# Edge attention on Trainium2: dividing the softmax on the edges and building the attention table with the edge pairs stationary

## What is computed

```python
Xq = (H @ W_lin.T).reshape(bt, n, h, dh)      # 4 heads of 64
Xv = (H @ W_val.T).reshape(bt, n, h, dh)
e = einsum('behd,hd->beh', leaky_relu(Xq[:, src] + Xq[:, dst], 0.2), a)
e = e + log(A0[src, dst] + 1e-8)[None, :, None]
e_t = e.transpose(1, 0, 2)
m = segment_max(e_t, src)
ex = exp(e_t - m[src])
attn = ex / segment_sum(ex, src)[src]
Y = segment_sum(attn[..., None] * Xv[:, dst], src)
return Y.reshape(bt, n, d) @ W_out.T
```

## Time and profile before

| | us |
|---|---|
| median of 3 runs | 2039.13 (2038.29 to 2039.25) |
| the profiled execution | 2038.4 |
| its span on the core | 2036.5 |
| edge attention, within it | about 1130 to 1637 |
| mean granted clock of TensorE | 0.984 |

### The profile page before, as it was taken

The page is one execution under the profiler, slowest core; times in us unless marked ns, Lnnn a source line. Parts: engine busy times, 40 slices in busy tenths (PEclk is TensorE's granted clock), DMA queues, the critical chain, the costliest instruction groups (busy, mean ns, idle before and its releaser), DMA issues. The chain is left out here.

```text
span 2036.5 us, 32320 instructions
## 1 busy us (share of the span) xinstructions
PE 1954.2 (96%) x11918; PEld 1586.9 (78%) x11918; DVE 1239.6 (61%) x2612; ACT 990.0 (49%) x1619; POOL 191.4 (9%) x162
## 2 busy tenths in 40 slices
PE   7999999999999999999999799999999889897998
PEld 6998888888888889888888556757565678686998
DVE  7454665544454535545554577575664588897786
ACT  3554564333332324322323365472736255675996
POOL 1000000001101010011011060000000011100000
PEclk8999999999999999999999899999999999997999
DMA  3111001000100000100102321422314131001232
GB/s 120 51 33 42 0 0 42 0 0 0 41 1 1 0 0 1 32 1 4 79 0 80 117 84 63 137 94 80 119 45 144 32 104 62 23 0 52 84 103 94
DMA packets 81490, 99.97 MB, mean 49 GB/s; under 512 B 7408, under 2 KB 73584, under 8 KB 79088
## 3 DMA queue, kind: packets, MB, share of 16 engines
q1 hardware_dynamic: 81392, 98.65, 14.7%
HBM read 61.78 MB, written 33.55 MB: 47 GB/s over the span
## 5 line engine op out<-in xcount | busy, mean ns | idle before, releaser
L706 ACT ACTIVATE b_gate<-b_pG,b_bias 128x512 f32<-128x512 f32 (+2 forms) x460 | 294.9, 669 | 368.5 <-PE b_pG L55 367.6
L53 PE MATMUL b_pG<-b_xshi,b_whi 128*128 128x512 f32 (+2 forms) x920 | 351.6, 382 | 2.3 <-PEq L299 1.4
L54 PE MATMUL b_pG<-b_xslo,b_whi 128*128 128x512 f32 (+2 forms) x920 | 351.3, 382 | 0.0
L55 PE MATMUL b_pG<-b_xshi,b_wlo 128*128 128x512 f32 (+2 forms) x920 | 351.3, 382 | 0.0
L756 DVE CAST b_xshi<-HT 128x512 fp32r<-128x512 f32 (+3 forms) x130 | 57.4, 484 | 285.2 <-PE b_pG L55 268.5
L53 PEld LDWEIGHTS b_pG<-b_xshi,b_whi 128*128 128x128 f32 x920 | 172.7, 188 | 35.7 <-issue 3.1
L54 PEld LDWEIGHTS b_pG<-b_xslo,b_whi 128*128 128x128 f32 x920 | 172.7, 188 | 32.4
L55 PEld LDWEIGHTS b_pG<-b_xshi,b_wlo 128*128 128x128 f32 x920 | 172.7, 188 | 32.2
L55 PE MATMUL b_pG<-b_hshi,b_wlo 128*128 128x512 f32 (+2 forms) x512 | 194.4, 380 | 0.0
L53 PE MATMUL b_pG<-b_hshi,b_whi 128*128 128x512 f32 (+2 forms) x512 | 194.4, 380 | 0.0
L54 PE MATMUL b_pG<-b_hslo,b_whi 128*128 128x512 f32 (+2 forms) x512 | 194.4, 380 | 0.0
(11 more groups left out here) (363 smaller groups left out, 3916.0 us busy)
## 6 DMA issues: line engine op xcount, KB each, us to landing
a_xt<-in_x SPq DMA_DIRECT2D x16, 512.0 KB, 5.8
h_scratch<-HT SPq DMA_DIRECT2D x4, 2048.0 KB, 7.0
l_x<-in_x SPq DMA_DIRECT2D x16, 512.0 KB, 3.4
l_w<-h_scratch SPq DMA_DIRECT2D x16, 512.0 KB, 5.1
x_scratch<-l_x SPq DMA_DIRECT2D x16, 512.0 KB, 3.2
c_x<-x_scratch SPq DMA_DIRECT2D x32, 256.0 KB, 3.6
x_scratch<-c_x SPq DMA_DIRECT2D x32, 256.0 KB, 2.6
l_x<-x_scratch SPq DMA_DIRECT2D x16, 512.0 KB, 3.7
```

The source lines that it names most:

```text
L53: nc.tensor.matmul(out, w_hi, x_hi, start=first, stop=False)
L54: nc.tensor.matmul(out, w_hi, x_lo, start=False, stop=False)
L55: return nc.tensor.matmul(out, w_lo, x_hi, start=False, stop=last)
L706: nc.scalar.activation(gate[s][:, g, 0:plan.n], pG[s][:, g, 0:plan.n], SIG[g], bias=bias[:, plan.p - 1, 2 * g + s:2 * g + s + 1])\
```

## The change

- Softmax is divided on the edges: four more steps on VectorE, all over 128x512. Step 4 is a scan that sums along a node's edges (restarting by the factor `keep`), step 5 a scan back that spreads each node's total, step 6 the reciprocal, step 7 the product with a bound on the reciprocal. `share` goes. `keep` is one copy made in `edge_cuts`.
- In the last group the steps are placed anew (`STEPS`), `exponent` moves from i = 5 to i = 4, `turn_linear` stands after the last `project`, and `turn_attention` with its split stands behind the last `score`. It waits for step 7.
- `fill` has the pairs of two source nodes stationary (128 columns) and the attention moving, high and low part side by side (256 columns). It gives the table with destination on the partitions at once: 16 matmuls for 4 pairs of nodes, eight times. Partition half b holds the sources of one half of each pair. `turn_full` goes. ScalarE copies the high product into by_dst and VectorE adds the low one (`add_low`); neighbours in both are 32 numbers apart in by_dst.
- by_dst is now (half of the pair, destination) by (graph and head) by 32 sources. So `sums` needs the values of a graph on both partition halves: 32 matmuls for 16, each with 32 moving columns for 64. SP copies values across the partition halves into `crossed` (two DMAs of 1 MB), which lies where relu's rows lie, after the last score (`scored`).
- The banks: `gather` uses three banks for four, `project` alternates between two for one, and waits for the tile before the last. Buffers in SBUF are placed anew.

```diff
@@ gather, project, score
-                    wait(pe, sem["s_lo"], QT * q + GT * m + (t if m else t - 1))
+                    wait(pe, sem["s_lo"], QT * q + GT * m + t - 1)
...
-                        wait(pe, sem["r_done"], KD * (gi - 2) + k + 1)
-                        nc.tensor.matmul(pZ[i % 2][:, k, :], keys[:, i, k * P:(k + 1) * P], tab["both"][:, :],
+                        wait(pe, sem["r_done"], KD * gi + k + 1 - NZ)
+                        nc.tensor.matmul(gathered(m, i, k), keys[:, i, k * P:(k + 1) * P], tab["both"][:, :],
                                          start=True, stop=True).then_inc(sem["z_mm"], 1)
@@ SyncE
+                    sp.wait_ge(sem["scored"], q + 1)
+                    if last:
+                        sp.wait_ge(sem["moved"], 32 * q)
+                    for own, other in (halves, halves[::-1]):
+                        sp.dma_start(crossed[other, :, :], vals[own, 0:QT, :]).then_inc(sem["crossed"], 16)
@@ fill, sums
-                    cols = slice(n * EDGES, (n + 1) * EDGES)
-                    for i, w in enumerate(weights):
-                        for c in range(EC):
-                            last = nc.tensor.matmul(pD[n % (2 * KD)], w[:, c, :], pairs[:, c, cols],
-                                                    start=i == 0 and c == 0, stop=i == 1 and c == EC - 1)
...
+                    if n >= 2:
+                        pe.wait_ge(sem["dst_done"], NF * q + n - 1)
+                    for i in range(FP):
+                        node = (FP * n + i) * P
+                        for c in range(EC):
+                            made = nc.tensor.matmul(pD[n % 2][:, i, :], pairs[:, c, node:node + P],
+                                                    weights[:, c, :, :].rearrange("p h s -> p (h s)"),
+                                                    start=c == 0, stop=c == EC - 1)
+                    made.then_inc(sem["full_mm"], 1)
...
-                                for g, r in enumerate(halves):
-                                    last = nc.tensor.matmul(pYT[h % 2][rows, g, k * P + u * NODES:k * P + (u + 1) * NODES],
-                                                            vals[r, t, head * DH:(head + 1) * DH],
-                                                            by_dst[r, SLOTS * k + 2 * t + i, :], start=True, stop=True)
+                                cols = slice(head * DH, (head + 1) * DH)
+                                for g in range(TILE_GRAPHS):
+                                    slot = NODES * g + SLOTS * k + 2 * t + i
+                                    at = HN * (TILE_GRAPHS * (HG // TILE_GRAPHS * k + u) + g)
+                                    for b, r in enumerate(halves):
+                                        last = nc.tensor.matmul(pYT[h % 2][rows, b, at:at + HN],
+                                                                (vals if b == g else crossed)[r, t, cols],
+                                                                by_dst[r, slot, :], start=True, stop=True)
@@ ScalarE
-                        act.wait_ge(sem["dst_mm"], NF * q + n + 1)
-                        nc.scalar.activation(by_dst[:, :, n * IF:(n + 1) * IF], pA[n % 2].rearrange("p (i s) -> p s i", s=NODES),
-                                             ACT.Copy).then_inc(sem["dst_done"], 1)
+                        act.wait_ge(sem["full_mm"], NF * q + n + 1)
+                        nc.scalar.activation(places(n), pD[n % 2][:, :, 0:P], ACT.Copy).then_inc(sem["dst_hi"], 1)
@@ VectorE
+                    if n == 4:
+                        dve.wait_ge(sem["exp_done"], q + 1)
+                        ins = V.tensor_tensor_scan(w[2], keep, w[1], 0.0, ALU.mult, ALU.add)
+                    if n == 5:
+                        ins = V.tensor_tensor_scan(w[3][:, ::-1], cut[:, EDGES:0:-1], w[2][:, ::-1], 0.0, ALU.add, ALU.max)
+                    if n == 6:
+                        ins = V.reciprocal(w[3], w[3])
+                    if n == 7:
+                        ins = V.scalar_tensor_tensor(out=w[1], in0=w[3], scalar=MOST, in1=w[1], op0=ALU.min, op1=ALU.mult)
...
+                def add_low(q, n):
+                    dve.wait_ge(sem["dst_hi"], NF * q + n + 1)
+                    V.tensor_tensor(places(n), pD[n % 2][:, :, P:2 * P], places(n), ALU.add).then_inc(sem["dst_done"], 1)
+
+                STEPS = ((1, 1), (2, 2), (2, 3), (5, 4), (6, 5), (7, 6), (7, 7))
```

More of the change, by code:

```diff
@@ L999, in edge_attention, with places, gathered @@
         NP = EC * 2
[L1000 to L1004, removed]
+        SOFT = 8
+        MOST = 1e30
         halves = (slice(0, NODES), slice(NODES, P))
+        def places(n):
+            return by_dst[:, :, n * FP:(n + 1) * FP].rearrange("p s i -> p i s")
         def lin_bank(m, part):
             return (pT if m else pZ[1])[:, part, :]
+        def gathered(m, i, k):
+            b = (KD * (GG * (m - 1) + i) + k) % NZ
+            return pZ[b // KD][:, b % KD, :]
         def bank(m, t):
-            return pE if m == 0 and t % 2 else pU
+            if t % 2 == 0:
+                return pU
+            return pZ[1][:, 1, :] if m else pE
         def halves_of(G, h):
@@ L1202, in score @@
                             rows = SLOTS * (2 * (i % 2) + k)
-                            nc.tensor.matmul(pE[rows:rows + SLOTS, :], tab["sign"][:, k, at:at + SLOTS],
-                                             relu_rows[i % RB][:, k, :], start=pair == 0, stop=False)
+                            last = nc.tensor.matmul(pE[rows:rows + SLOTS, :], tab["sign"][:, k, at:at + SLOTS],
+                                                    relu_rows[i % RB][:, k, :], start=pair == 0, stop=False)
+                    if end:
+                        last.then_inc(sem["scored"], 1)
                 def add_linear(q):
@@ L1215, in turn_attention, with fill @@
                     last.then_inc(sem["at_mm"], 1)
-                def fill(q, n):
+                def fill(q, n, last):
                     if n == 0:
@@ L1304, in body @@
                         group(q, m, NJ if last else 2 * NJ)
-                    score(q, top, GG // 2 - 1)
+                    score(q, top, GG // 2 - 1, end=True)
                     if last:
                         add_linear(q)
-                        turn_attention(q)
-                    fill(q, 0)
-                    fill(q, 1)
-                    for n in range(2, NF):
-                        fill(q, n)
-                        turn_full(q, n - 2, last)
-                    turn_full(q, NF - 2, last)
-                    turn_full(q, NF - 1, last)
+                    turn_attention(q)
+                    for n in range(NF):
+                        fill(q, n, last)
                     sums(q, 0)
@@ L1592, in group @@
                                     part(q, n)
-                        if m == NJ and i == 2:
-                            softmax_step(q, 1)
-                        if m == NJ and i == 4:
-                            softmax_step(q, 2)
-                            softmax_step(q, 3)
+                        if m == NJ:
+                            for at, step in STEPS:
+                                if i == at:
+                                    softmax_step(q, step)
                 def body(q, last=False):
```

97 lines of the change are left out of this document (37 added, 60 removed).

## The result

The changed kernel takes **2065.25 us** (median of 4 runs, 2063.26 to 2067.93) where the kernel before takes 2039.19 in the same comparison (2038.29 to 2039.7). The ratio is 1.0128, with a 95% interval of 1.0116 to 1.014: 26 us slower. The forecast was slower by 16, to 2055, with a range of 2036 to 2077: the time lies inside the range, but above the 2047 to 2062 that the forecast itself was given. The profiled executions have spans of 2063.0 and 2036.5 us, 26.5 apart, and what follows accounts for these.

A forecast was written before the change was run, and what follows sets the result against it. PE, busy 96% of the span, was taken as the bound. Passes 0 to 2 at +4.75 us each (14.3), the last pass +2.3 and the first group -0.5 made +16 on 2039.1: 2055 us, range 2036 to 2077.

The forecast's parts named there:

- Strided writes set the fill: Rival: ScalarE 1.08 and VectorE 1.5 make fill rounds 2.4 us each, giving 2071 us; chance 0.11.
- Start of the fill: Last score to fill: softmax steps on VectorE delay fill by 7.65 us in passes 0 to 2, 6.6 in the last.
- the 1.4: End of the last group: VectorE's reductions begin 1.4 us later, since turn_linear stands behind the last project.
- the 2.7 us: Between product and fill: from first transpose of the attention to first fill, 2.69 us in the trace's last pass.
- A cheap reciprocal: Rival in the softmax: the reciprocal takes 0.69 us, 10.6 us go, 2037 if the clock holds; chance 0.12.
- The fill: Fill with tail and clock: 18.0 + 1.9 - 25.17 = -5.25 us in passes 0 to 2, -7.15 in the last.
- PE sets the pace: Fill rounds: two buffers turn in 3.9 us, just under PE's two rounds of 4.0, so PE sets the pace.
- The clock: Behind the hole before the fill in passes 0 to 2: clock at half, costing fill 1.9 us, transposes 0.5.
- Sums: Sums: doubled 64-column loads at 15 ns a pass cost +0.48 us a half step, +3.85 a pass over 32 graphs.
- Two tiles overlap only: Rival in sums: 29 ns a pass, +1.38 us a half step, 2084 us; chance 0.10.
- Groups: Gather, project, score: project's second bank removes waits for keys, -1.5 us a pass, -1.0 in the last.
- Before and behind: Ahead of pass 0's last score: -2.0 us from three free groups and the first group; behind the last sums: 0.

The follow-up runs named there:

- no_recip: Changed kernel with the softmax reciprocal replaced by a multiplication by one over the same 128x512, division left out: 2052.51 us.
- busy_hole: Changed kernel with useless 512-column matmuls in the holes, 22 ahead of the turn of the attention (48 in the last pass), 6 behind it: 2056.02 us.
- dense-rows run: Changed kernel with by_dst laid out node first, so the fill writes dense rows and sums read moving columns at 512 B steps: 2058.64 us.
- half_loads: Changed kernel with stationary tiles of 32 for 64 columns in the 64 passes of a half step of sums: 2063.8 us.
- half_columns: Changed kernel with 16 for 32 moving columns in each of the 64 passes of a half step of sums: 2072.07 us.
- banks_alone: Kernel before with only the change of PSUM banks in the groups (gather over three, projections alternating between two): 2034.54 us against 2039.33.
- log_division: Changed kernel with the softmax division done in the exponent (ScalarE logarithm, VectorE subtraction, ScalarE exp), no reciprocal or product: 2055.35 us.

## Why the prediction was right in direction and 10 us short

In short: two thirds of what was missing is one step, the pace of the fill. The range held because it took in the rival "Strided writes set the fill", whose mechanism is what the runs showed.

**Start of the fill: right.** Passes 0 to 2 lost 7.65 us each, forecast 7.65, and the last 6.71 for 6.6. The slope of two small reciprocals gave 3.35 us, and 3352 ns was measured. The steps behind it agree too: from the last score, VectorE's reductions begin after 18.6 us and the product ends after 24.85, both as forecast. That the sum agrees to the hundredth is luck, since terms like the 1.4 and the 2.7 us in it were given to a tenth. By "VectorE: DVE Perf Modes" of the Trainium skill, section "First, the fixed hardware budget", with its repeat count of 8, the estimate was 4.3 us; the trace's 3.352 speaks for about 6.25 ns an element (3352 less 203 over 504), and the measurement decides. The rival "A cheap reciprocal" falls by the same row, and no_recip shows what a pass of 0.43 us there would gain.

**The fill: the step that failed.** The term was -5.25 a pass and came out at -3.5 to -3.8, and -4.5 for -7.15 in the last: 7.5 us of the 10.4 that were missing. The formula held: two rounds take PE's 2.08, the copy, the add and 0.15. The step that failed is its result, "PE sets the pace", because two prices in it were mis-sized. ScalarE's strided copy was put at 0.60, its dense time, though the bound of 1.08 stood beside it, and took 1.08. VectorE's add was put at 1.08 and took 1.18. With these the formula gives 2.08 + 1.08 + 1.18 + 0.15 = 4.49 us, and 4.50 and 4.57 were measured. Three such pairs of rounds, a last pair at PE's 4.0 and a tail of 0.16 + 1.08 + 1.18 + 0.15 = 2.57 make 20.0 us a pass, which is what busy_hole shows at full clock (19.9 to 20.1). The forecast said "PE sets the pace, with nothing to spare"; with nothing to spare, each tenth on a price counts three times and once more in the tail of a pass, 16 times in all. At full clock the step is thus 8.1 us short; the clock's own part of the fill, put at 1.9 us a pass, came out below that in passes 0 to 2 (1.2 to 1.7), which hides some of it. The rival "Strided writes set the fill", at 0.11, had the mechanism, with too high a price for VectorE (1.5), so that its 2071 is too slow by 6. The dense-rows run shows it: without the strides PE's wait between rounds goes, and the four fills lose 12.0 us.

**The clock: right where it was looked for.** It falls at the end of each new hole, for 6.8 us in passes 0 to 2. That it costs time was shown by busy_hole: 1.7 to 2.2 us a pass with the way to the fill, where 2.4 were forecast (1.9 and some 0.5). The forecast missed the last pass, which had been slow before: a longer hole (11.39 us for 4.69) has the clock low for 17 us there, not 6.8, of which 9 lie in the hole itself and 5 in the fill, and it falls again in its first sums, 0.8 us.

**Sums: right.** +0.48 us a half step was forecast, 0.46 measured (2.71 less 2.25), and 64 passes start within 0.94 us, 15 ns each. A pass over 32 graphs came out at +3.24 for +3.85, since the first two half steps together cost only 0.49 (4.30 us to the third's start for 3.81): the forecast charged all eight. half_loads and half_columns show that the loads set it. "Two tiles overlap only" falls: it would need 29 ns a pass. The Trainium skill's page "TensorE: Matmul & The Clock Gate", section "Wait — 56ns, not 53.3ns?", gives a floor of about 25 ns between starts; across four tiles this trace has 15, and the measurement decides.

**Groups: right.** -1.38, -1.32 and -1.80 for -1.5, -1.5 and -1.0, and banks_alone (-1.30, -1.28 and -1.77) shows that the banks do it.

**Before and behind: not forecast.** 4.0 us ahead of the first last score (+1.96 for -2.0) and 1.0 behind the layer are another 5.0 us; the sums and groups, 2.1 us cheaper than forecast, hide part of it. The two go with the granted clock, which is low for 17.0 us between 1145 and 1200 us, for 10.2 before, and for longer behind the layer too. They are not a step of the forecast as far as the runs show: of ten traces with the changed early part or nearly that, six are 0.4 to 2.6 us faster there than the kernel before, where -2.0 was forecast. Why the clock was low for longer in this one stays open.

## What to carry to other kernels

When a pace is a sum of steps on several engines that comes out within a few per cent of another engine's pace, price each step by the nearest row of the same access pattern, and where there is none, take the dear end. A hole in TensorE's stream can cost more than its length: here, without useless work in it, each hole of 2.5 to 5.4 us before the fill had the clock at half for 3.4 to 10.3 us, and a kernel with less work (half the columns) lost for that reason alone. So read the pace of a stage between starts at full clock, and not from the kernel's time. Try the parts of a change that only remove a wait by themselves; here the change of banks, which needs nothing of the rest, made the old kernel faster.

## What the runs showed of the hardware

- VectorE's reciprocal: 3352 ns over 512 elements a partition (203 over 8), where the product behind it takes 690 and a scan 1225.
- Writes with 128 B from one element to the next: ScalarE 1081 ns for 598, VectorE 1178 for 691, 0.48 and 0.49 us more over 512 elements.
- TensorE reading 32 moving columns 512 B apart instead of side by side: 64 passes in 1.13 us for 0.94.
- fp32 passes on 64 by 64 tiles start every 15 ns whether 16 or 32 columns move, and every 10 ns with loads of 32 columns (64 in 0.62 us, on tiles of 64 by 32).
- ScalarE loads a table for 1283 ns at each change between logarithm and exponent, eight times in four passes (log_division).
- VectorE beside GpSimd's work on edge_pairs: 3.73 us for a pass over 512 elements in three traces, where the next such pass of the changed kernel takes 0.43.
- Two DMAs of 1 MB from one partition half to the other land 9.2 us after issue, against 5.6 for one over all partitions. They stayed hidden, as forecast.

```profile
c_relu<-c_vals SPq DMA_DIRECT2D x8, 1024.0 KB, 9.2
```
